# Four cross-attention layers on one core: PSUM banks divided two and five, value products in blocks of two, layer 2's scores in f16 parts

## What is computed

```python
# layer 0 (layers 1 and 3 alike, with biases and a layer norm after the residual)
xn, kvn = rmsnorm(x, gq), rmsnorm(ctx, gkv)
q, k, v = heads(xn @ wq.T), heads(kvn @ wk.T), heads(kvn @ wv.T)
attn = softmax(einsum('bshd,bkhd->bhsk', q, k) * 8 ** -0.5)
x = xn + einsum('bhsk,bkhd->bshd', attn, v).reshape(B, S, 128) @ wo.T + bo
# layer 2
scores = einsum('bhqd,bhkd->bhqk', Q, K) / 8 ** 0.5
sim = softmax(where(causal, scores, -1e9))
a = layer_norm(einsum('bhqk,bhkd->bqhd', sim, V).reshape(B, S, 128) + x)
x = gelu(a @ W1.T + b1) @ W2.T + b2 + a
```

## Time and profile before

| | |
|---|---|
| median of 3 runs | 1093.32 us (1092.89 to 1095.54) |
| the profiled execution | 1095.62 us, its span on the core 1093.7 us |
| TensorE busy | 975.5 us, 89% |
| VectorE, ScalarE, GpSimd busy | 840.1, 726.5 and 339.6 us |
| mean granted TensorE clock | 0.972 of full |
| chain that ended last | TensorE 60%, VectorE 25%, ScalarE 6% |

### The profile page before, as it was taken

One profiled execution on the slowest core, in us unless ns is written; L12 is line 12 of the kernel. 1 busy time (PEld: TensorE's weight loads), 2 busy tenths in 40 slices (PEclk: granted clock), 3 DMA queues, 4 the chain that ended last, 5 costly groups with the idle time before them and its releaser, 6 DMA issues.

```text
span 1093.7 us, 43761 instructions
## 1 busy us (share of the span) xinstructions
PE 975.5 (89%) x18794; PEld 580.6 (53%) x18794; DVE 840.1 (77%) x1783; ACT 726.5 (66%) x1636; POOL 339.6 (31%) x363
## 2 busy tenths in 40 slices
PE   0679999999989999999999998999999899999996
PEld 0245555555545555555555555655555565655653
...
GB/s 214 71 82 84 57 57 84 74 53 83 51 69 84 85 61 84 100 75 85 84 102 18 100 17 95 31 71 31 84 28 76 52 54 84 21 81 50 55 5 5
DMA packets 63640, 73.74 MB, mean 67 GB/s; under 512 B 8130, under 2 KB 59114, under 8 KB 63318
## 3 DMA queue, kind: packets, MB, share of 16 engines
...
## 4 chain that ended last, share of the span: by engine, by line
PE 60%; DVE 25%; ACT 6%; issue 6%; POOL 1%; SPq 1%; DMA 0%; POOLq 0%; ACTq 0%; DVEq 0%
PE ring L573 23%; PE sexp L573 13%; PE acc L741 13%; DVE mx L1124 10%; PE ring L616 4%; DVE mneg L1130 4%; DVE mx L1122 3%; ACT probs L983 2%; DVE kp L1101 2%; PE ring L805 2%; PE ring L795 1%; PE ring L593 1%; SPq L457 1%; PE ring L752 1%; DVE ssq L1086 1%
## 5 line engine op out<-in xcount | busy, mean ns | idle before, releaser
L1124 DVE TENSOR_TENSOR mx<-ring,mx 120x400 f16<-120x400 f32 (+1 forms) x1056 | 564.8, 566 | 165.7 <-PE ring L573 160.7
L983 ACT ACTIVATE probs<-sexp 120x400 f32<-120x400 f32 (+1 forms) x1152 | 536.4, 514 | 179.8 <-PE sexp L573 176.3
L573 PE MATMUL ring<-qx,krep 96*32 96x400 f16 (+2 forms) x4608 | 416.1, 349 | 16.4 <-DVE oatt L1176 5.7
L573 PE MATMUL sexp<-qx,krep 97*32 97x400 f16 (+2 forms) x4608 | 410.7, 343 | 12.4 <-ACT probs L983 7.2
L741 PE MATMUL acc<-probs,vx 120*18 120x200 f32 (+1 forms) x4608 | 257.6, 340 | 0.8 <-ACT probs L983 0.7
L573 PEld LDWEIGHTS sexp<-qx,krep 97*32 97x32 f16 (+2 forms) x4608 | 132.5, 97 | 110.0 <-ACT probs L983 40.1
L573 PEld LDWEIGHTS ring<-qx,krep 96*32 96x32 f16 (+2 forms) x4608 | 134.9, 99 | 103.4 <-DVE mx L1124 13.4
L741 PEld LDWEIGHTS acc<-probs,vx 120*18 120x18 f32 (+1 forms) x4608 | 136.0, 100 | 67.5 <-issue 8.7
L508 POOL TENSOR_TENSOR qx<-qs,headmask 96x400 f16<-96x400 f16 x96 | 79.7, 858 | 287.2 <-DVE qs L1111 287.2
L573 PE MATMUL ring<-ct,wk 128*32 128x480 f16 (+1 forms) x864 | 60.4, 387 | 25.6 <-DVE oatt L1176 10.5
L480 POOL TENSOR_TENSOR ct<-ctf,ct 128x480 f16<-128x480 f32 (+1 forms) x72 | 80.7, 1121 | 5.8
...
## 6 DMA issues: line engine op xcount, KB each, us to landing
...
```

The lines of the kernel that those rows point to most:

```text
L573: last = run(out[g:g + m], w[:, g:g + m], x, **flags)
L983: act.activation(probs[0:r, j % PR, :], sexp[j % SR][0:r, 0:QW], ACT.Exp).then_inc(sem["probs_ready"], 1)
L1124: op = dve.tensor_tensor(dst, src, dst, ALU.max)
```

## The change

`SR`, `RING` and `TOGETHER` become 2, 5 and 2, and `VALUES_AT` follows. `place` keeps for each bank an expected release, from a table `HOLD` of durations in steps, and takes the bank with the smallest. VectorE's `maximum` waits besides for its own tile four earlier. In layer 2 `k2` and `q2` are split into an f16 part and a remainder, the spread keys are made of both parts, and a score tile is the sum of three f16 products. The value products of layer 2 take the form of the other layers' (`a2`, two heads a matmul), are copied to `osb2` by ScalarE and transposed back (`o2`), and VectorE reads them as it reads O.

```diff
-PR, SR, RING = 10, 3, 4
+PR, SR, RING = 10, 2, 5
-       "pt0": 31, "pt1": 33, "pt2": 34, "pt3": 35, "o": 43, "out": 45}
+       "pt0": 31, "pt1": 33, "pt2": 34, "pt3": 35, "a": 42, "o": 44, "out": 45}
+HOLD = {"smax": 1.6, "k": 3.0, "v": 2.0, "ct": 2.0, "O": 2.8, "q": 2.6, "xT": 1.6, "mt": 2.6, "mn": 1.6, "OT": 1.8,
+        "wo": 1.8, "mk": 2.0, "cx": 1.8, "kqv": 3.0, "s": 1.8, "pt": 1.8, "a": 1.8, "o": 3.0, "at": 1.8, "h": 6.0, "w": 1.8,
+        "flag": 2.0}
-TOGETHER = 4
+TOGETHER = 2
...
+        free_at = [0.0] * RING
         def place(s, n):
             for j in range(NSTEP):
                 m = max_tile(s, j)
                 uses = [(f"smax{m[1]}", m[0])] if m is not None else []
-                for use in uses + other_products(s, n, j):
-                    SLOT[key(*use)] = len(SLOT) % RING
+                for i, (use, u) in enumerate(uses + other_products(s, n, j)):
+                    slot = min(range(RING), key=lambda k: free_at[k])
+                    SLOT[key(use, u)] = slot
+                    now = max(NSTEP * n + j + 0.25 * i, free_at[slot])
+                    free_at[slot] = now + HOLD[use.rstrip("0123456789")]
...
                 pool.wait_ge(*at("kqv2_read", u, 1))
-                pool.tensor_tensor(kbd2[:, :, :], k2[:, :].unsqueeze(1).broadcast_to([128, H, S]),
-                                   heads[:, :].unsqueeze(2).broadcast_to([128, H, S]), ALU.mult
-                                   ).then_inc(sem["kbd2_ready"], 1)
+                pool.tensor_copy(kq16[:, 0, :, :], k2[:, :, :]).then_inc(sem["kq2_high"], 1)
+                pool.wait_ge(*at("kq2_high", u, 1))
+                pool.tensor_tensor(kq16[:, 1, :, :], k2[:, :, :], kq16[:, 0, :, :], ALU.subtract).then_inc(sem["kq2_low"], 1)
+                pool.wait_ge(*at("kq2_low", u, 1))
+                for i in range(2):
+                    last = pool.tensor_tensor(kbd2[:, i, :, :], kq16[:, i, 0, :].unsqueeze(1).broadcast_to([128, H, S]),
+                                              heads16[:, :].unsqueeze(2).broadcast_to([128, H, S]), ALU.mult)
+                last.then_inc(sem["kbd2_ready"], 1)
...
-                grouped(pe.matmul, ps[0:S, 0:QW], q2[:, :], kbd2[:, HT * t:HT * t + HT, :].rearrange("p h s -> p (h s)"),
-                        start=True, stop=True).then_inc(sem["s2_filled"], 1)
+                for i, (a, b) in enumerate(((0, 0), (1, 0), (0, 1))):
+                    last = grouped(pe.matmul, ps[0:S, 0:QW], kq16[:, a, 1, :],
+                                   kbd2[:, b, HT * t:HT * t + HT, :].rearrange("p h s -> p (h s)"),
+                                   start=(i == 0), stop=(i == 2), skip_group_check=True)
+                last.then_inc(sem["s2_filled"], 1)
...
+            def values2(u):
+                pe.wait_ge(*at("pt2_read", u, T))
+                ps = begin("a2", u)
+                for side in range(2):
+                    for q in range(4):
+                        h = 8 * side + 2 * q
+                        last = pe.matmul(ps[32 * q:32 * q + VW, 2 * S * side:2 * S * side + 2 * S],
...
+            def output2(u):
+                pe.wait_ge(*at("a2_read", u, 1))
+                ps = begin("o2", u)
+                for t in range(T):
+                    last = pe.transpose(ps[0:S, 128 * t:128 * t + 128], osb2[:, S * t:S * t + S], ident[:, :])
+                last.then_inc(sem["o2_filled"], 1)
...
                 dve.wait_ge(*at("smax_ready", u, i + 1))
+                if c > 0:
+                    dve.wait_ge(*at("smax_used", u, i - T + 1))
```

57 lines of the change are left out of this document (33 added, 24 removed), and 4 rows, old and new, of the table PER.

## The result

The changed kernel takes 1083.07 us (median of 4 runs, 1081.63 to 1084.95) against 1093.57 for the kernel before on the same chip: a ratio of 0.990, 95% interval 0.989 to 0.992, a gain of about 10.5 us. I had forecast 1072, a gain of 21. The sign and the range were right; the gain was half of what I said. The profiled execution has a span of 1083.1 us.

What follows compares the result with a forecast made beforehand. It took TensorE as the bound, with VectorE and ScalarE close and 5 to 8 us of waits a stage. Terms -18 - 53 + 27 + 27 - 4 = -21 took 1093.3 to 1072 us (1062 to 1084; full range 1046 to 1101).

Steps and rivals of the forecast that it cites:

- Blocks of two: Value products in blocks of two steps, not four: same instructions, spread finer, VectorE's added wait long over; 0 us.
- Layer 2's work: TensorE in layer 2: f16 scores and value products by columns save about 2.3 us in eight stages, -18 us.
- Fifth bank: A fifth bank for tiles other than the exponentials' removes TensorE's waits on banks still being read: -53 us.
- second bank: Exponentials' scores with two banks, not three: ScalarE's other instructions between exponentials now show as TensorE waits, +27 us.
- GpSimd's chain: GpSimd's longer key spreading in layer 2, from 2.9 to 6.5 us, delays VectorE: +27 us, bounds +5 and +36.
- the stopped VectorE instruction: In layer 2, oatt plus a bias row, with two SBUF inputs, stops beside GpSimd's long multiplication, losing some 2 us.
- the root: GpSimd's feed-forward square root, queued behind layer 2's key spreading, comes 3.6 us later, so VectorE waits.
- Rival 4: GpSimd's long layer-2 multiplications take 3.4 us each: nine us more, 1081; chance 0.10.
- The clock: Layer 2's low-clock stretches after 9-column value blocks go, three of five at 1.3 us: -4 us, bounds -13 to +8.
- rival 2: The exponentials' loop becomes the bound, interruptions of ScalarE paid in full: slower, +40, 1112 us; chance 0.18.
- Rival 3: Waits only move: TensorE's gain in layers 0 and 1 returns at the end of the maxima, 1087; chance 0.12.
- Rival 1: In layer 2, five banks cover GpSimd's longer work: +5 in place of +27, 1050 us; chance 0.17.

Runs made afterwards that it cites:

- x_acc1: The changed kernel with ScalarE copying the accumulator out two exponentials earlier (`ACC_AT` 1, not 3): 1059.55 us, ratio 0.968 to the kernel before.
- x_first5: The changed kernel with each unit's first value block moved from step 3 to step 5, ScalarE's order untouched: 1063.07 us, ratio 0.972 to the kernel before.
- x_layer2: The kernel before with the new layer 2 alone (three and four banks in turn, blocks of four): 1084.64 us, ratio 0.992.
- x_acc1_three: x_acc1 with three banks for the exponentials and four for the rest, in place of two and five: 1067.03 us, ratio 0.974 to the kernel before.
- x_release: The kernel before with its four banks given out by expected release instead of in turn, and VectorE's added wait: 1092.17 us, ratio 0.999.
- x_acc1_root: x_acc1 with GpSimd's square root for the feed-forward unit ahead of layer 2's key-spreading instructions: 1057.88 us, ratio 0.966 to the kernel before.

## Why the prediction was wrong in size

**The step that failed** is "Blocks of two", which I costed at nothing: "Same instructions, spread finer". I had looked at the blocks' ends and at VectorE's wait, not at where the first block of a unit now stands. It costs 23.5 us (x_acc1; 20.0 by x_first5), about the whole gain that I forecast. The wait stands in a function that the diff does not touch, and only `VALUES_AT` moves its place by three steps.

With that alone put right my sum would say 1072 + 23.5 = 1095.5, and the kernel takes 1083. So the other terms were too dark by 12 us. That the forecast came within 11 us is in part luck: an error of 23.5 one way and one of 12 the other. Term by term:

- **Layer 2's work, -18: right.** TensorE is busy 2.24 us less a stage in x_layer2; I took 2.3.
- **Fifth bank and second bank, -53 and +27: right in layer 2, of the wrong sign elsewhere, as far as release order goes.** In layer 2, without the chain, the net is -2.4 us a stage and 15 in all (forecast -2.3 and 18). In layers 0 and 1 it is +0.4 and +0.9 (x_acc1_three to x_acc1), where I had -1.0 and -0.5, and in the last stage +5.2, where I had +1.5. The waits of the earlier trace rows did go, but they go with four banks in release order too (x_release has none at O's reader and 0.9 us at the keys'), and others come in their place. Layers 0 and 1 of x_acc1 are faster by 10.9 us than before, and the order and the smaller blocks give 14.4 with the banks as they were; my -8 for these eleven stages was near by luck. The two terms apart no run shows.
- **Blocks of two, 0: wrong a second time, the other way.** Apart from the wait, they go with 6.9 us less in layers 0 and 1 with three banks and 10.9 with two. So the price of the second bank hangs on the block size: from three and four banks to two and five, these stages lose 3.5 us with blocks of two, and 7.5 with blocks of four (417.8 in x_release to 425.3, ScalarE's wait for the last block included).
- **GpSimd's chain, +27: right in kind, too large.** It is 47.23 to 45.10, 2.1 us a stage where I had 2.9 to 3.9. That is 17 us in all by stages, 15 by the times, 12 by the ratios. Of my two causes the stopped VectorE instruction has the most, and the root 1.7 by the times, which is within the noise, or 2.6 by the stages. My texts did not agree on that share: the prediction leaves 19 of the 27 with the root, the expectation of x_acc1_root a third. Rival 4 is out: the multiplications take 2.86 us each (5.72 for two), not 3.4.
- **The clock, -4: right in size, by another road.** In layer 2 the clock stood at 0.50 for 27.3 us before and for 13.7 in the changed kernel; at 1.2 us for each 3.4 that is 4.8 us. The stretches behind the 9-column blocks are all gone, and four new ones came. I had read the eight stages as 48.9 to 50.1 us; the longest, with a low stretch of 10.2 us, has 55.6. In x_acc1 3.4 us of low clock are left in layer 2, some 8 us less than before.
- **Not in the sum:** 3.1 us before the first stage ends (128.77 to 125.69). Kernels with blocks of two and three exponentials' banks have 126.9 to 129.0 there, those with two 122.6 to 126.4, so it goes with the banks; by which wait I did not look into.

The changed kernel without the wait is x_acc1. Its profiled execution is 36.4 us shorter than that of before, and my sum said 21. Cut into the same parts, the sum is missed by 3.7 us before the first stage ends, by 1.4 each in layer 0 and layer 1, by 9.9 in layer 2 and by 0.9 behind it, all too dark, and by 1.3 the other way in the last stage. In layer 2 the chain (10 us) and the clock (4) are more than enough, the banks take 3 back, and about 1 us stays open.

Of the rivals, rival 2 (the exponentials' loop) did not happen as a slower kernel, but its mechanism is there: TensorE is idle for 21.7 us before exponentials' products in x_acc1, 7.2 in the kernel before, and 61.0 with blocks of four. Rival 3 named nearly the right time (1087) for the wrong reason: the gains of layers 0 and 1 were handed back, not at the maxima but at the accumulator. Rival 1 did not happen either: x_acc1 comes into its range (1040 to 1062) with the chain's 15 us still in it, through the order, the blocks, the clock and the start. What I wrote under what would break it, a late reader behind which a product stands, was the right kind of thing; I looked for it in the ring's slots only, and the accumulator is a ring of one.
